# Attention with a feed-forward layer on one core: units of a key head as 3, 2, 1, 4, 5, 8, 6, 7 key blocks, and halves of keys and values split behind the fourth score product of the long steps

## What is computed

```python
xn = layernorm(x)                                  # x: 2 x 1024 x 512
q = rope(xn @ Wq.T)                                # 32 heads of 128
k = [rope part: xn @ Wkr.T | rest: c_kv @ Wupk.T]  # 8 key heads of 128, c_kv = xn @ Wdk.T
v = c_kv @ Wupv.T                                  # 8 value heads of 128
attn = softmax(causal(q @ k.T / sqrt(128)))        # 4 query heads to a key head
out = x + (attn @ v) @ Wo.T + (silu(xn @ Wg.T) * (xn @ Wu.T)) @ Wd.T
```

## Time and profile before

| | us |
|---|---|
| median of 3 runs | 2233.33 (2232.90 to 2233.84) |
| the profiled execution | 2236.64 |
| its span, first to last instruction | 2234.8 |
| first query product of attention | 537.6 |
| one key head in the middle, from S(0,0) to the next S(0,0) | 104.63 |
| PE busy | 2201.1, 98% of the span |
| DVE, ACT, POOL busy | 1609.4, 1129.3, 945.3 |

### The profile page before, as it was taken

How to read it: one execution, slowest core, us unless ns; L and a number is a source line. 1 busy time by engine, 2 the same in 40 slices (tenths; PEclk the granted TensorE clock), 3 DMA queues, 4 the chain that set the end, 5 groups by cost and what they waited for, 6 DMA issues and landing times.

```text
span 2234.8 us, 33748 instructions
## 1 busy us (share of the span) xinstructions
PE 2201.1 (98%) x11776; PEld 1304.0 (58%) x11776; DVE 1609.4 (72%) x3732; ACT 1129.3 (51%) x2232; POOL 945.3 (42%) x807
## 2 busy tenths in 40 slices
PE   8999999999999999999999999999999999999998
PEld 6667575765555555555555555555555555555554
DVE  5665554546778787878777777878787878777765
ACT  3323425344555555555455555555555555555644
POOL 4001010102545455555455545555454555455542
PEclk9999999999999999999999999999999999999999
DMA  5756568487111102010202131211101010202000
GB/s 198 287 158 231 201 167 278 160 300 262 29 45 37 55 22 58 24 57 20 62 18 62 44 100 53 72 52 29 57 20 57 24 57 20 62 22 60 15 29 20
DMA packets 82088, 196.89 MB, mean 88 GB/s; under 512 B 9216, under 2 KB 25984, under 8 KB 75264
## 3 DMA queue, kind: packets, MB, share of 16 engines
q1 hardware_dynamic: 79808, 190.55, 27.2%
q10 hardware_dynamic: 2112, 4.19, 0.5%
HBM read 148.57 MB, written 46.14 MB: 87 GB/s over the span
## 4 chain that ended last, share of the span: by engine, by line
PE 90%; DVE 4%; issue 2%; ACT 2%; DMA 1%; POOL 1%; DVEq 0%; SPq 0%; ACTq 0%
PE ob L1418 17%; PE scores L1390 15%; PE qb L1368 13%; PE ob L1429 13%; PE ptb L1402 11%; PE ring L1124 8%; PE ring L1144 8%; PE down L1155 4%; PE ring L1181 2%; DVE acc L1339 1%; ACT short_prob L1262 1%; DVE q_sin L1317 1%; DMA ff_raw<-in_ffw 1%; ACT oT L1279 1%; DVE q_cos L1319 1%
## 5 line engine op out<-in xcount | busy, mean ns | idle before, releaser
L1276 ACT ACTIVATE pT<-ptb 128x512 f16<-128x512 f32 x576 | 332.5, 589 | 343.9 <-PE ptb L1402 342.2
L1418 PE MATMUL ob<-pT,v 128*128 128x512 f16 x1728 | 437.9, 379 | 1.2
L1323 DVE SCALAR_TENSOR_TENSOR pT<-ptb,pT 128x512 f16<-128x512 f32 x576 | 390.3, 687 | 54.8 <-ACT pT L1276 46.9
L1241 POOL TENSOR_TENSOR long_prob<-long_prob,rinv 128x384 f32<-128x384 f32 (+3 forms) x256 | 303.3, 1200 | 132.7 <-DVE rinv L1346 132.6
L1429 PE MATMUL ob<-wo,oT 128*128 128x512 f16 x1536 | 352.9, 379 | 3.6 <-DVE oT L1327 3.6
L1247 POOL TENSOR_TENSOR q_cos<-q_cos,q_sin 128x512 f32<-128x512 f32 x124 | 157.5, 1270 | 461.3 <-DVE q_cos L1319 461.3
L1368 PE MATMUL qb<-xT,wq 128*128 128x512 f16 x1488 | 349.1, 379 | 0.0
L1241 POOL TENSOR_TENSOR short_prob<-short_prob,rinv 128x512 f32<-128x512 f32 (+3 forms) x256 | 276.1, 1094 | 156.8 <-DVE rinv L1346 156.8
L1390 PE MATMUL scores<-kT,late_qT 128*128 128x384 f16 (+3 forms) x1536 | 313.0, 340 | 5.3 <-DVE nmax L1302 4.7
L1262 ACT ACTIVATE long_prob<-long_prob,nmax 128x384 f32<-128x384 f32 (+3 forms) x256 | 204.8, 800 | 183.1 <-DVE nmax L1302 180.3
L1262 ACT ACTIVATE short_prob<-short_prob,nmax 128x512 f32<-128x512 f32 (+3 forms) x256 | 190.8, 745 | 154.7 <-DVE nmax L1302 154.7
(11 more groups left out here) (119 smaller groups left out, 2751.3 us busy)
## 6 DMA issues: line engine op xcount, KB each, us to landing
wq<-w_halves SPq DMA_DIRECT2D x126, 256.0 KB, 3.2
ff_raw<-in_ffw SPq DMA_DIRECT2D x56, 384.0 KB, 5.9
w_fetch<-in_wqo SPq DMA_DIRECT2D x16, 1024.0 KB, 7.1
w_fetch<-in_wqo SPq DMA_DIRECT2D x32, 512.0 KB, 4.8
w_halves<-w_parts SPq DMA_DIRECT2D x32, 512.0 KB, 3.1
wo<-w_halves SPq DMA_DIRECT2D x16, 1024.0 KB, 5.0
k_rows<-stage SPq DMA_DIRECT2D x128, 64.0 KB, 1.7
v_rows<-stage SPq DMA_DIRECT2D x32, 256.0 KB, 2.3
```

What stands on the lines that cost most here:

```text
L1241: nc.gpsimd.tensor_tensor(prob[n % 2][:, h, 0:W], prob[n % 2][:, h, 0:W], rinv[:, hd % 8:hd % 8 + 1].broadcast_to([P, W]), ALU.mult)\
L1276: nc.scalar.activation(pT[:, t % 4, HI], ptb[t % 2][:], ACT.Copy, scale=P_SCALE).then_inc(pT_hi, 1)
L1323: nc.vector.scalar_tensor_tensor(pT[:, t % 4, LO], ptb[t % 2][:], P_SCALE, pT[:, t % 4, HI], ALU.mult, ALU.subtract).then_inc(pT_split, 1)
L1418: mm = nc.tensor.matmul(ob[:], v16[e % 2][:, x, j], pT[:, t % 4, y], start=(j == 0 and (x, y) == (HI, HI)), stop=(is_last(kind, n, j) and ...
```

## The change

Three tables are changed, and no instruction is added or taken away.

- `ORDER`: the places 0 to 7 now have 3, 2, 1, 4, 5, 8, 6, 7 key blocks.
- `PIECES` in place of `K_UNITS, V_UNITS`: the K halves become ready behind S(5,3) and S(6,3), the v halves behind S(7,3) and behind S(0,3) of the head in which they are used (the first PV with them stands in step 1).
- The costs of the planner are others: the delays after DVE's S and INV are longer, after EXP shorter, the products of PE a little cheaper.

```diff
-K_UNITS, V_UNITS = (4, 5), (6, 7)
+PIECES = {(5, 3): ("K", 0), (6, 3): ("K", 1), (7, 3): ("V", 0), (0, 3): ("V", 1)}
...
-ORDER = (3, 2, 1, 0, 4, 6, 5, 7)
+ORDER = (2, 1, 0, 3, 4, 7, 5, 6)
...
-        return [("dve", "S", n, j, 1.04 * cols + 0.08, 0.1), ("act", "EXP", n, j, 0.98 * cols + 0.15, 0.2),
-                ("dve", "INV", n, j, 0.12, 0.06), ("pool", "NORM", n, j, 1.83 * cols + 0.03, 0.05)]
+        return [("dve", "S", n, j, 1.04 * cols + 0.14, 0.14), ("act", "EXP", n, j, 0.98 * cols + 0.28, 0.08),
+                ("dve", "INV", n, j, 0.09, 0.1), ("pool", "NORM", n, j, 1.83 * cols + 0.06, 0.1)]
...
-    ge, pos = n // TB + 1, n % TB
-    if kind == "S" and j == 0 and ge < B * KVH:
-        for units, hi, lo in ((K_UNITS, "KH", "KL"), (V_UNITS, "VH", "VL")):
-            if pos in units:
-                half = units.index(pos)
-                return [("act", hi, ge, half, 0.6, 0.1), ("dve", lo, ge, half, 0.95, 0.1)]
+    ge = n // TB + (n % TB > 0)
+    if kind == "S" and (n % TB, j) in PIECES and 0 < ge < B * KVH:
+        what, half = PIECES[n % TB, j]
+        return [("act", what + "H", ge, half, 0.6, 0.1), ("dve", what + "L", ge, half, 0.95, 0.1)]
...
-        return max(3 * key_blocks(n) * P * 0.00045, 0.33)
+        return 3 * key_blocks(n) * P / 2400 + 0.01
```

More of the change, by code:

```diff
@@ L198, in followers @@
     if kind == "S":
-        return [("dve", "S", n, j, 1.04 * cols + 0.08, 0.1), ("act", "EXP", n, j, 0.98 * cols + 0.15, 0.2),
-                ("dve", "INV", n, j, 0.12, 0.06), ("pool", "NORM", n, j, 1.83 * cols + 0.03, 0.05)]
+        return [("dve", "S", n, j, 1.04 * cols + 0.14, 0.14), ("act", "EXP", n, j, 0.98 * cols + 0.28, 0.08),
+                ("dve", "INV", n, j, 0.09, 0.1), ("pool", "NORM", n, j, 1.83 * cols + 0.06, 0.1)]
     if kind == "Q":
-        return [("dve", "Q", n, j, 1.97, 0.05), ("pool", "Q", n, j, 1.1, 0.1),
-                ("act", "QL", n, j, 0.55, 0.1), ("pool", "QL", n, j, 1.1, 0.1)]
+        return [("dve", "Q", n, j, 2.02, 0.08), ("pool", "Q", n, j, 1.24, 0.1),
+                ("act", "QL", n, j, 0.56, 0.1), ("pool", "QL", n, j, 1.13, 0.1)]
     if kind == "W":
-        return [("dve", "W", n, j, 0.61, 0.1)]
+        return [("dve", "W", n, j, 0.66, 0.1)]
     if kind == "T" or is_last(kind, n, j):
-        return [("act", kind, n, j, 0.53, 0.08), ("dve", kind, n, j, 0.61, 0.1)]
+        return [("act", kind, n, j, 0.54, 0.1), ("dve", kind, n, j, 0.62, 0.1)]
     return []
 def pieces_split(kind, n, j):
-    ge, pos = n // TB + 1, n % TB
-    if kind == "S" and j == 0 and ge < B * KVH:
-        for units, hi, lo in ((K_UNITS, "KH", "KL"), (V_UNITS, "VH", "VL")):
-            if pos in units:
-                half = units.index(pos)
-                return [("act", hi, ge, half, 0.6, 0.1), ("dve", lo, ge, half, 0.95, 0.1)]
+    ge = n // TB + (n % TB > 0)
+    if kind == "S" and (n % TB, j) in PIECES and 0 < ge < B * KVH:
+        what, half = PIECES[n % TB, j]
+        return [("act", what + "H", ge, half, 0.6, 0.1), ("dve", what + "L", ge, half, 0.95, 0.1)]
     return []
@@ L244, in product_cost @@
     if kind == "S":
-        return max(3 * key_blocks(n) * P * 0.00045, 0.33)
+        return 3 * key_blocks(n) * P / 2400 + 0.01
     if kind in ("QF", "Q"):
         part = q_part(kind, n)
-        return (part[1] - part[0]) * 0.68
-    return {"T": 0.44, "PV": 0.72, "W": 2.72}[kind]
+        return (part[1] - part[0]) * 0.648
+    return {"T": 0.436, "PV": 0.648, "W": 2.592}[kind]
 def orders():
```

## The result

The changed kernel takes **2239.14 us** (median of 19 runs, 2237.30 to 2241.32) where the kernel before takes 2233.33 (19 runs, 2231.70 to 2238.57): a ratio of **1.0025**, interval 1.0018 to 1.0032 (ratios are taken over all runs and not between the medians). That is slower by a quarter of a per cent, 5.8 us in the medians. The forecast was 2236.6, in a range of 2228 to 2243. The time lies in the range, and the two new waits that were forecast are there. But the effect is 5.8 us and not 3.3, and the outcome that I held likeliest (within 0.2%) is not the one measured.

The account below looks back on a forecast made before the run. PE was busy 98% of the span, so only its waits (31.4 us) could move the time. Middle heads +7.3, first head -0.8 and last -3.2 gave +3.3 on the median 2233.33: 2236.6 us, range 2228 to 2243.

Parts of the forecast that it names:

- S(4,3), -0.47, T(4,0), -0.03: Middle heads: with the key half gone from step 4, these two waits of PE vanish, 0.47 and 0.03 us a head.
- S(3,3), +0.11: Middle heads, 4-key-block step behind the 1-block one: this score product waits 0.11 us for DVE's S(3,1).
- Third pass of PV(2,0), +0.46: Middle heads: PV's third pass waits 0.46 us for T's low part, queued on DVE behind S(3,2).
- T(5,0), +0.42: Middle heads, 8-block unit: DVE's key half delays POOL's NORM(5,2), so this transpose starts 0.42 us late.
- The middle heads, +7.3: Waits of 1.26 us a head against 0.74, +0.52 in each of 14 heads: 7.3 us slower.
- The first head, -0.8, and the last, -3.2: Waits fall from 9.7 to 8.9 us in the first head and from 11.3 to 8.1 in the last.
- The base: The starting time to which the +3.3 us was added: the runs' median 2233.33 us, not the profiled execution's 2236.64.
- (a): Rival: DVE and POOL don't get in each other's way here, T(5,0) waits for nothing, 6.3 us less: 2230.3; chance 0.13.
- (b): Rival: the plan holds and PV's third pass isn't late either, 7.4 us less: 2222.9, faster; chance 0.08.
- (c): Rival: POOL gets in first, T(5,0) starts 0.8 us late instead of 0.42: 2241.9, slower; chance 0.08.
- (d): Rival: the clock falls at S(0,3) or the last head's T(5,0), 1.7 us each, up to 2240.0; chance 0.13.
- (e): Rival: overlooked waits, each spare 0.1 us that turns into 0.2 costing 3 us in 15 heads; chance 0.14.

Follow-up runs that it names:

- half_early: The changed kernel with each next head's first key half moved to behind T(4,0) on ACT and DVE, where POOL is idle: 2233.09 us, ratio 0.9997.
- half_last: The changed kernel with the low part of the first key half moved behind INV(5,3) on DVE: 2239.29 us, ratio 1.0025.
- costs_only: The kernel before with only the planner's new costs, old unit sequence and old places for the halves: ratio 1.0000.
- pieces_only: The kernel before with only the key and v halves at their new places, old unit sequence and old costs: 2232.07 us, ratio 0.9988.

## Why the prediction was right where it was, and where it was not

- **S(4,3), -0.47, T(4,0), -0.03.** Right: both gone. That a wait stood behind S(4,3) for the old sequence (T(4,0), 0.26) didn't enter here, but would have for the halves alone.
- **S(3,3), +0.11.** 0.03 in thirteen of the middle heads, 0.11 in the first and the ninth alone: mis-sized, by about 1 us over all. The third pass of PV behind it takes half of that back: 0.50 where S(3,3) waits 0.03.
- **Third pass of PV(2,0), +0.46.** Right, 0.50, and from DVE's L1321 as said.
- **T(5,0), +0.42.** Right, 0.43, and its cause too: half_early takes the half away and the wait with it. The two NORMs end at 1031.52 + 4.17 = 1035.69, and the second, 1.89 long, overlaps the first by 0.04; so NORM(5,2) ended at 1033.84, 3.97 behind S(5,3), forecast 4.00. That is 1.75 behind the half's end at 1031.36 + 0.73 = 1032.09, which is NORM's length less 0.14; the operation of the earlier trace rows gave the same, 1.15 behind with a length of 1.29. The Trainium skill (SBUF — State Buffer, Who interferes with whom) has the later of the two fully blocked until the first is through; with NORM's 1.89 that would be 1.89 behind the half, and the two traces here (the changed kernel and half_last) show 1.75; the measurement decides.
- **The middle heads, +7.3.** 14 x (1.23 - 0.74) = +6.9.
- **The first head, -0.8, and the last, -3.2.** This is the step that failed. By the traces without a fall the first went from 8.8 to 8.6 and the last from 9.6 to 8.3, together -1.5 instead of -4.0. What the changed kernel has there was near (8.9 and 8.1 forecast, 17.0 together; 16.9 measured). What I took off was not always the kernel's: I read a fall of the clock at two places of one execution, 1.69 us of lost time at each, and booked the two as waits that the kernel before always has. In a second trace of it there is none, behind the same waits, and its waits in the two heads are 0.9 and 1.7 shorter. The sum with the right terms is +6.9 - 0.2 - 1.3 = +5.4; measured are 5.8 in the medians and 5.6 in the lowest runs.
- **The base.** The profiled execution lay 3.3 us above the median, and I called that chance and went on from the median. Two falls were in that execution, while more than half of the kernel's runs elsewhere (16 of 29) have a mean clock of 1.000: taking the terms from the one and the base from the other is what lost the 2.5 us. The excess was itself the hint. The forecast of 2239.9 for an execution like the profiled one lies near the measured median of 2239.14, but by luck: it compares a kernel with two falls and one with none.
- **Rivals.** (a), (b) and (c) are refuted by the rows: one NORM in four is longer, PV's third pass is late, and the half starts 0.16 us ahead of NORM. (d) is open: neither of two traces of the changed kernel has a fall, at S(0,3), at the last head's T(5,0) or elsewhere, but 6 of 19 of its runs have a mean clock of 0.998, some 3 us above those with 1.000. half_early shows where it can fall: behind the wait of 2.11 us at S(1,2), which the forecast has (2.3 with that of S(1,3)) and takes to leave the clock alone. (e) didn't come: in the middle heads the one wait that the forecast had overlooked is 0.04 at the second matmul of T(7,4), in step 0 of the next head, and the 0.03 that it had put at T(0,2) is not there. The chances put the border between "same" and "slower" right beside the forecast, and the time fell on its other side, by 0.05%.

## What to carry to other kernels

Before a term is booked as a saving, look whether a second execution of the kernel has it: a fall of TensorE's clock, above all, may be of the run. Where an operation hides behind ACT and DVE, look what POOL is doing at that moment, and where a list is the work of a planner, look at the two operations next to each moved one; here a few instructions moved within the lists brought the changed kernel some 13 us, and to 0.9963 of the kernel before, where the three parts of the change alone came to between 0.9988 and 1.0003. And a removed wait is worth what it had beyond the next one: 0.24 of 0.47 and 0.24 of 0.50 here.

## What the runs showed of the hardware

- The clock's falls differ between executions of the same program: in two traces of the kernel before, after the same wait of 2.77 us, TensorE ran on at 2.4 GHz in one and fell to 1.2 GHz (a mean of 0.54 over 3.5 us) in the other. Of the thirteen traces four have such a fall in attention: before, costs_only, half_early and pieces_only. Of the kernel before and of the changed one, runs with a mean clock of 0.998 took some 3 to 4 us more than those with 1.000.
- When DVE's half (two inputs in SBUF, 0.74 us) and the next of POOL's NORMs were both waiting for the NORM before to end, DVE got in first (half_last). A half that waited so ended 0.55 us behind the NORM in two traces (1242.90 behind 1242.35, 1239.59 behind 1239.05), and a NORM that waited for a half ended 1.75 behind it (the changed kernel and half_last): the half 0.19 and the NORM 0.14 less than its own length. Why is open; spans of POOL are rough.
- Attention began between 535.3 and 538.2 us in the traces, with the same program ahead of it: nearly 3 us of difference between executions that no list of this change touches. It was not followed up.
